# Deformable stage: samples of two 4x4 half blocks side by side on the partitions, and one tile more of lead for the preparation

## The reference, cut to what matters

```python
def deform_conv2d(x, offset, mask, weight):          # K = 3, STRIDE = PAD = 1
    ...
    py = hs + ky + dy                                # row of tap k, plus its offset
    px = ws + kx + dx
    y0 = jnp.floor(py)
    x0 = jnp.floor(px)
    ...
    val = gather(y0i, x0i) * w00 + gather(y0i, x0i + 1) * w01 + gather(y0i + 1, x0i) * w10 + gather(y0i + 1, x0i + 1) * w11
    w_r = weight.reshape(weight.shape[0], weight.shape[1], K2)
    out = jnp.einsum('bkhwc,bkhw,ock->bohw', val, mask, w_r)
    return out
offset = conv2d(x, offset_w, offset_b)
mask = jax.nn.sigmoid(conv2d(x, mask_w, mask_b))
...
x = x + _L1_conv_ref(_gn(x), L1_conv_offset_w, L1_conv_offset_b, L1_conv_mask_w, L1_conv_mask_b, L1_conv_dcn_w)
```

## Time and profile before

| what | us |
|---|---|
| median of 3 runs | 2346.87 |
| the three runs | 2318.73, 2346.87, 2351.54 |
| the profiled execution, its own time | 2314.87 |
| its span | 2313.1 |
| attention, to about | 860 |
| the deformable stage, first spread to last contraction | 911 to 1572 |
| Fourier and FFT convolution | 1583 to 2313 |

### The profile page before, as it was taken

One profiled execution on the slowest core, in us unless ns is written; L12 is line 12 of the kernel. 1 busy time (PEld: TensorE's weight loads), 2 busy tenths in 40 slices (PEclk: granted clock), 3 DMA queues, 4 the chain that ended last, 5 costly groups with the idle time before them and its releaser, 6 DMA issues. The chain is left out here.

```text
span 2313.1 us, 46229 instructions
## 1 busy us (share of the span) xinstructions
PE 2045.3 (88%) x14981; PEld 1256.5 (54%) x14981; DVE 1281.6 (55%) x2688; ACT 1133.4 (49%) x3617; POOL 788.5 (34%) x743
## 2 busy tenths in 40 slices
PE   5699999999999963999999999995694999999999
PEld 3566666666666641232333333324682877777776
DVE  5178888888888871555555555555336222222222
ACT  2378888888888853555555555540121111111111
POOL 0178788787887841222222222210000110110110
PEclk9889999999999985898898998887777999999999
DMA  4300000000000015444444444415002112112110
GB/s 165 110 25 27 26 24 27 26 28 26 26 27 26 24 45 144 123 133 127 121 126 120 123 133 129 108 47 91 10 10 66 34 34 66 33 33 65 34 33 14
DMA packets 169883, 149.70 MB, mean 65 GB/s; under 512 B 60645, under 2 KB 159563, under 8 KB 169694
## 3 DMA queue, kind: packets, MB, share of 16 engines
q1 hardware_dynamic: 169774, 148.38, 24.2%
HBM read 83.68 MB, written 45.89 MB: 56 GB/s over the span
## 5 line engine op out<-in xcount | busy, mean ns | idle before, releaser
L412 ACT ACTIVATE at_probs<-at_sc,at_nmx 128x196 f32<-128x196 f32 x1152 | 473.7, 424 | 116.9 <-DVE at_nmx L358 114.8
L340 POOL TENSOR_TENSOR at_probs<-at_probs,at_rs 128x784 f32<-128x784 f32 x288 | 429.9, 1493 | 156.6 <-DVE at_rs L363 156.6
L447 PE MATMUL at_pt<-at_ident,at_probs 128*98 128x128 f32 x2304 | 312.7, 279 | 40.7 <-DVE at_pts L368 40.1
L358 DVE TENSOR_REDUCE at_nmx<-at_sc 128x4 f32<-128x784 f32 x288 | 277.7, 964 | 124.7 <-PE at_sc L436 124.7
L1237 ACT ACTIVATE dn_mix<-dn_mps 128x432 f32<-128x432 f32 x384 | 182.6, 527 | 297.3 <-PE dn_mps L1139 296.8
L447 PEld LDWEIGHTS at_pt<-at_ident,at_probs 128*98 128x98 f32 x2304 | 242.0, 129 | 142.2 <-POOL at_probs L340 78.6
L436 PE MATMUL at_sc<-at_kw,at_qw 32*128 32x196 f32 x2304 | 273.5, 357 | 12.0 <-POOL at_qw L329 8.0
L1330 DVE COPY dn_sampled<-dn_sps 128x432 f32<-128x432 f32 x192 | 116.7, 608 | 252.3 <-PE dn_sps L1150 251.4
L1139 PE MATMUL dn_mps<-dn_stack,dn_selw 42*128 42x432 f16 x768 | 199.0, 383 | 52.9 <-DMA dn_stack<-near_corners 47.4
L1323 DVE TENSOR_SCALAR dn_mix<-dn_mps 128x432 f32<-128x432 f32 x384 | 213.8, 598 | 44.4 <-PE dn_mps L1139 44.4
L2014 PE MATMUL fc_qps<-fc_wk,fc_xs 99*128 99x128 f32 x1728 | 207.9, 277 | 31.6 <-DMA fc_xs<-in_ones 31.6
(11 more groups left out here) (153 smaller groups left out, 2397.6 us busy)
## 6 DMA issues: line engine op xcount, KB each, us to landing
fc_xs<-fc_xp SPq DMA_DIRECT2D x144, 120.0 KB
dn_slab<-near_image SPq DMA_DIRECT2D x72, 200.0 KB, 3.7
at_vs<-attention_values SPq DMA_DIRECT2D x288, 49.0 KB
near_corners<-dn_split SPq DMA_DIRECT2D x24, 486.0 KB
dn_stack<-near_corners SPq DMA_DIRECT2D x24, 486.0 KB
dn_patch<-near_pixels SPq DMA_DIRECT2D x24, 384.0 KB
attention_values<-ap_vrow SPq DMA_DIRECT2D x21, 256.0 KB, 2.3
near_image<-dn_chunk SPq DMA_DIRECT2D x24, 200.0 KB, 1.9
```

What stands on the lines that cost most here:

```text
L340: nc.gpsimd.tensor_tensor(probs[s][p][:, :, :, :], probs[s][p][:, :, :, :], rs[s][:, 2 * p:2 * p + 2, :].unsqueeze(3).broadcast_to([P, 2, ...
L358: nc.vector.tensor_reduce(nmx[s][:, 2 * p:2 * p + 2, :], sc[p][:, :, 0:2 * NK].rearrange("p b (j k) -> p b j k", j=2), AX.X, ALU.max, nega ...
L412: nc.scalar.activation(probs[s][p][:, b, j, :], sc[p][:, b, NK * j:NK * j + NK], ACT.Exp, bias=nmx[s][:, 2 * p + b, j:j + 1], accum_out=su ...
L447: mm = nc.tensor.transpose(pt[b % 2][0:HK, o:o + P], probs[s][p][:, b % 2, j, HK * c:HK * c + HK], ident[:, :])
```

## The change

The block of 4 x 12 pixels becomes two half blocks of 4 x 4 that share the partitions: partitions 0 to 63 hold the 8 x 8 patch of the left half block, 64 to 127 that of the right one. A tile is then 12 blocks of 8 columns, and a step takes three of them (`PER`), so a tile has 4 steps of 432 columns instead of 8. `stack` has 36 rows of data (18 for each half) over 16 constant rows and is loaded by two DMAs; `spread` still is four matmuls of 432 columns a step. `sample` becomes 3 blocks x 4 images x 2 halves, each a matmul of 64 rows x 32 columns by 144, into two banks `sps0`, `sps1`. `keep` is done for each half. `turn` moves into the bank `cps` of `conv`, with waits between the two. The maps are stored by image and tap, so that one DMA loads all three replicas, and `bias_maps` and `residual` are two instructions each.

The preparation gets one more tile of lead: in tile t, PE convolves tile t+3 in steps 0 and 1 (before: steps 5 to 7), ACT makes the corner weights of t+2 wholly in tile t, `high(t+2)` included (before: `high(t+1)` in step 2), and SP stores the corners of t+1 at the head of its list for tile t (before: at its end).

```diff
-DBW = 12
-DSTEPS = W // DBW
-COLS = TAPS * DR * DBW
-PATCH = (DR + 4) * (DBW + 4)
+HBW = 4
+DBW = 2 * HBW
+NBLK = W // DBW
+PER = 3
+DSTEPS = NBLK // PER
+PX = DR * HBW
+COLS = PER * TAPS * PX
+REACH = HBW + 4
+PATCH = 2 * (DR + 4) * REACH
...
-DATA = 18
-STACK = DATA + DR + 4 + DBW + 4
+DATA = 36
+STACK = DATA + DR + 4 + REACH
...
             def load_patch(j):
...
+                side = (DR + 4) * REACH
+                sp.dma_start(patch[j % 2][0:side, :, :].rearrange("p k n -> p (k n)"),
+                             rows[:, :, 0:NBLK, :].rearrange("r q k n -> (r q) (k n)")).then_inc(patch_in[j % 2], 16)
+                for i in range(2):
+                    sp.dma_start(patch[j % 2][side + i * side // 2:side + (i + 1) * side // 2, :, :].rearrange("p k n -> p (k n)"),
+                                 rows[:, HBW * (1 - i):HBW * (2 - i), i:NBLK + i, :].rearrange("r q k n -> r q (k n)")).then_inc(patch_in[j % 2], 16)
...
             def load_maps(j):
...
-                for a, to in enumerate((hat_y, off_x, mask)):
-                    sp.dma_start(to[:, :], map_d[j % 2, TAPS * a:TAPS * a + TAPS, :, :].rearrange("k b n -> (k b) n").unsqueeze(1).broadcast_to([TAPS * B, 3, DPX])
-                                 ).then_inc(rep_in, 16)
+                sp.dma_start(offs[:, :, :].rearrange("p a n -> p (a n)"),
+                             map_d[j % 2, :, :, :].rearrange("b (k a) n -> (b k) (a n)", a=3).unsqueeze(1).broadcast_to([B * TAPS, 3, 3 * DPX])).then_inc(rep_in, 16)
...
             def load_stack(j):
                 sp.wait_ge(corners_out, 16 * (j + 1))
+                if j >= 1:
+                    sp.wait_ge(stack_in, 32 * j)
...
+                for h in range(2):
+                    sp.dma_start(stack[j % 2][DATA // 2 * h:DATA // 2 * (h + 1), :, :, :, :].rearrange("p b t k n -> p (b t) (k n)"),
+                                 corner_d[j % 2, :, :].rearrange("(g r) (e n) -> (r e) g n", r=3, n=DPX)[:, :, DPX // 2 * h:DPX // 2 * (h + 1)]).then_inc(stack_in, 16)
...
@@ SP, the loop over tiles
             for t in range(DTILES):
                 if t + 1 < DTILES:
+                    store_corners(t + 1)
                     load_patch(t + 1)
+                if t + 1 < DTILES:
+                    load_stack(t + 1)
+                if t + 4 < DTILES:
+                    load_slab(t + 4)
                 save(t)
-                if t + 2 < DTILES:
-                    store_maps(t + 2)
                 if t + 3 < DTILES:
-                    load_slab(t + 3)
+                    store_maps(t + 3)
+                if t + 6 < DTILES:
+                    store_image(t + 6)
+                if t + 3 < DTILES:
+                    load_maps(t + 3)
                 if t + 4 < DTILES:
                     store_pixels(t + 4)
-                if t + 5 < DTILES:
-                    store_image(t + 5)
-                if t + 2 < DTILES:
-                    load_maps(t + 2)
-                if t + 1 < DTILES:
-                    store_corners(t + 1)
-                    load_stack(t + 1)
...
@@ PE
             def turn(g):
...
+                if g >= 2:
+                    pe.wait_ge(maps_ready, 2 * g if g >= 4 else 2 * g - 2)
...
             def sample(s):
...
-                for b in range(B):
-                    mm = nc.tensor.matmul(sps[C * b:C * b + C, 0:COLS], patch[t % 2][:, k, C * b:C * b + C], mix[s % 2][b][:, :], start=True, stop=True)
+                side, n = PATCH // 2, TAPS * PX
+                for i in range(PER):
+                    for b in range(B):
+                        for h in range(2):
+                            mm = nc.tensor.matmul(sps[h][C * b:C * b + C, n * i:n * i + n], patch[t % 2][side * h:side * h + side, PER * k + i, C * b:C * b + C],
+                                                  mix[s % 2][b][side * h:side * h + side, n * i:n * i + n], start=True, stop=True)
...
-                    if k == 0 and t + 4 < DTILES:
+                    if t + 3 < DTILES:
+                        for kx in ((0, 1), (2,), (), ())[k]:
+                            conv(t + 3, kx)
+                    if k == 2 and t + 4 < DTILES:
                         turn(t + 4)
                     if t >= 1:
-                        for tap in range(2 * k - 2, 2 * k):
-                            if 0 <= tap < TAPS:
-                                contract(t - 1, tap)
-                    if t + 3 < DTILES and k >= 5:
-                        conv(t + 3, k - 5)
+                        for tap in ((), (0, 1), (2, 3, 4), (5, 6, 7, 8))[k]:
+                            contract(t - 1, tap)
@@ ACT, in step k of tile t
-                    if t + 2 < DTILES and k == 0:
-                        bias_maps(t + 2)
-                    if t + 1 < DTILES and k == 2:
-                        high(t + 1)
-                    if t + 2 < DTILES and k >= 4:
-                        prepare(t + 2, k - 4)
+                    if k == 1 and t + 3 < DTILES:
+                        bias_maps(t + 3)
+                    if t + 2 < DTILES:
+                        for part in ((0, 1), (2,), (3,), ())[k]:
+                            prepare(t + 2, part)
+                        if k == 3:
+                            high(t + 2)
@@ DVE
-            def keep(s):
+            def keep(s, h):
...
+                nc.vector.tensor_copy(sampled[t % 2][:, :, h, PER * PX * k:PER * PX * (k + 1)].rearrange("p t (k n) -> p t k n", k=PER),
+                                      sps[h][:, 0:COLS].rearrange("p (k t n) -> p t k n", k=PER, t=TAPS)).then_inc(mix_dve, 1)
...
+                    if k == 1 and t + 6 < DTILES:
+                        normalise(t + 6)
+                    if k == 2 and t + 4 < DTILES:
                         keep_rows(t + 4)
-                    if k == 1 and t + 5 < DTILES:
-                        normalise(t + 5)
-                    if k == 2 and t + 2 < DTILES:
-                        largest(t + 2)
-                    keep(s)
-                    if k == 6 and t >= 1:
+                    if k == 3 and t + 3 < DTILES:
+                        largest(t + 3)
+                    for h in range(2):
+                        keep(s, h)
+                    if k == 3 and t >= 1:
                         residual(t - 1)
```

More of the change, by code:

```diff
@@ L949, in stage_deform_near @@
         ident = sb("ident", [P, P])
-        stack = [sb(f"stack{i}", [STACK, TAPS, B, 3 * DR, THIRD], F16) for i in range(2)]
+        stack = [sb(f"stack{i}", [STACK, B, TAPS, NBLK, PX], F16) for i in range(2)]
         stage_stats(nc, "gn1", x_sb, agg,
@@ L1251, in _ @@
             bias_maps(0)
+            prepare(0, 0)
             bias_maps(1)
-            for part in range(4):
+            for part in range(1, 4):
                 prepare(0, part)
             high(0)
+            bias_maps(2)
             for part in range(4):
                 prepare(1, part)
+            high(1)
             for b in (2, 3):
@@ L1347, in _ @@
             largest(1)
+            largest(2)
             for b in range(2):
@@ L1380, in host_l1d @@
     bias = np.zeros((B, C), np.float32)
-    bias[:, 0:27] = np.stack([ob[0::2], ob[1::2], mb]).reshape(27)
+    bias[:, 0:27] = np.stack([ob[0::2], ob[1::2], mb], 1).reshape(27)
     caps = np.zeros((B, C), np.float32)
-    caps[:, 0:18] = 2
+    caps[:, 0:27:3] = 2
+    caps[:, 1:27:3] = 2
     taps = dw.reshape(C, C, TAPS)
@@ L1388, in host_l1d @@
     p = np.arange(PATCH)
-    main = (DR + 4) * DBW
-    r = np.where(p < main, p // DBW, (p - main) // 4)
-    q = np.where(p < main, p % DBW, DBW + (p - main) % 4)
+    side = PATCH // 2
+    u = (p - side) % (side // 2)
+    r = np.where(p < side, p // REACH, u // HBW)
+    q = np.where(p < side, p % REACH, HBW * ((p - side) // (side // 2)) + u % HBW)
     sel = np.zeros((STACK, PATCH), np.float16)
-    for rho in range(3):
-        for half in range(2):
-            for sigma in range(3):
-                sel[6 * rho + 3 * half + sigma, (r % 3 == rho) & (q % 3 == sigma)] = UNIT ** -2
+    for h in range(2):
+        for rho in range(3):
+            for half in range(2):
+                for sigma in range(3):
+                    sel[DATA // 2 * h + 6 * rho + 3 * half + sigma, (p // side == h) & (r % 3 == rho) & (q % 3 == sigma)] = UNIT ** -2
     sel[DATA + r, p] = 1
```

132 lines of the change are left out of this document (65 added, 67 removed).

## The result

The changed kernel takes **2206.95 us** (median of four executions, 2195.37 to 2232.31) against 2336.07 for the kernel before (four executions by then), a ratio of 0.943 with a 95% interval of 0.933 to 0.954. Run again beside the experiments it took 2205.23 (2185.81 to 2224.05), the kernel before 2321.46 in 13 executions there: 0.945 (0.936 to 0.954). Some executions of every kernel are some per cent longer at a lower granted clock; the ratios are taken without them, the medians with them. So it is faster, inside the range, but the forecast was 2130: about three fifths of the expected gain came (129 us between the medians above, 217 forecast).

The account below looks back on a forecast made before the run. PE bounded the old kernel; afterwards the stack chain (17.4 us) plus 0.8 for low clock makes 18.2 us a tile, the stage 437 instead of 644. With 4 for the start, 2112, plus 16 for the median: 2130 us, range 2070 to 2235.

Parts of the forecast that it names:

- TensorE's tile of 15.7 us: PE's work per tile at full clock: spread 3.3, contraction 6.4, convolution 2.0, transposes 0.6, sampling 3.4 us.
- the price by instruction: Rival on sampling: 48 matmuls at 57 ns, 2.7 us a step, PE's tile up to 23.2; chance 0.16 including turn-taking.
- taking turns: Rival on sampling: the two row halves do not overlap, slot 1.6 us, PE's tile 18.7; chance 0.16 including instruction pricing.
- The stack next: With PE's tile shortened, the chain leading to the next stack's load binds; PE waits 1.7 us for each stack.
- 17.4 us: Length of the chain from a tile's first spread through relus, rounding, corner store and stack load to the next tile's.
- SP comes to the store some tenths late: Small addition to the stack chain: the maps load ahead of the corner store waits for corner weights, five pixel stores follow.
- off SP's queue, not off the path: The maps' load as one issue instead of three saves SP 1.6 us, counted as not shortening the stack chain.
- SP's list eats it: No-gain rival: SP's issue list, or a wait between turn and conv, keeps the tile at 26 us, 2317; chance 0.03.
- the packet rival: Stack load priced by packets: 1296 of 384 bytes take 4.5 us longer, chain 21.5, kernel 2209 us; chance 0.12.
- The 16 us for the median: Half of the 32 us between profiled execution and three-run median, added to 2112 to give 2130.
- the rival of a clock that stays at 1.2 GHz: Waits for every stack keep PE's clock low: tile 29.3 us, kernel 2396, 2% over the median; chance 0.04.
- the cheaper case: Rival: the stack chain hides, PE alone sets 15.8 to 16.5 us a tile, about 2080 us; chance 0.10.

Follow-up runs that it names:

- doubled sampling: Against the changed kernel, each sampling matmul is issued twice into the same place; 2205.19 us, ratio 0.952 to the kernel before.
- slab later: Against the changed kernel, SP issues the convolution's slab load just before the maps load, not right behind the stack load; 2161.86 us, ratio 0.931 to the kernel before.
- stack ahead of patch: Against the changed kernel, stack load right behind the corner store, before the patch; rounding before the relus; slab, image and pixel stores moved; 2177.22 us, ratio 0.933.
- all waits covered: Against the changed kernel, rounding before the relus; SP order behind the stack: maps store, image store, slab, save, pixel stores, map load; 2166.89 us, ratio 0.935.

## Why the prediction was right, and where it was short

- **TensorE's tile of 15.7 us**: right. The sampling slot is 0.92 us; the price by instruction (2.7) and taking turns (1.6) are out, and without the stack loads TensorE is busy for 15.7 us a tile at a granted clock of 0.98, in a tile of 16.6. The estimate from the Trainium skill's 60 cycles a matmul ("TensorEngine Tiling (Array Packing)", Performance Considerations), 1.2 us a step, is refuted by the same 0.92.
- **The stack next**: right as to what TensorE waits for, wrong as to why, and mis-sized. The term "17.4 us" took the load at 6.5 us; it is 10.2, and the patch loads, 9 to 12 us behind the stack in the old kernel, now stand right ahead of it; with the stack ahead of them it was 6.8 where TensorE waited. "SP comes to the store some tenths late" is 2.5 us in the tile shown. And the chain is not the bound: cut, it leaves the tile as it was.
- **The failed step** is thus that the sum had no term for SP's queue. I gave its issues away as "off SP's queue, not off the path", though the chain of the earlier trace rows passes through it twice. At 26.8 us a tile it had slack (182.9 us of waiting for TensorE), at 18.2 it had none. The rival "SP's list eats it" named the place, with 26 us too high a price and 0.03 too low a chance.
- **Two terms mis-sized**: the tile of 21.7 us is 17.9 in which TensorE is busy and 3.9 in which it is not. Over the 15.7 at full clock the busy part is 2.2 us, where the forecast had 0.8 for stretches at 1.2 GHz; the rest is the stack, where it had 1.7. But as SP sets the pace, a full clock alone would mostly lengthen the wait: doubled sampling, at a higher clock, left the tile almost as it was.
- **Sum**: 3.4 us a tile too few are 82 us; the first sampling matmul came 9 to 10 us later instead of 4 (3.7 us of that had piled up before the stage, by the end of its statistics). 2112 + 82 + 6 = 2200, and the second profiled execution is 2201.90. The first has the 29 us of the Fourier stretch on top. That 2207 lies in the range is partly luck: the tile of 17 to 19.5 us, which had 0.55, did not come, the upper end of the range was drawn for a dearer sampling, and the packet rival hits the number (2209) by a mechanism that is refuted.
- **The 16 us for the median** were not there: in 13 executions the kernel before has 2321.46, 6.6 above its profiled one, so the three executions lay high.
- **Low clock**: 0.87 granted, against 0.88 before; the rival of a clock that stays at 1.2 GHz is out. So are packets, the cheaper case and no gain. Two readings in these rivals were off, without weight here. "Within some ten us each time" holds in some cases only: in the kernel before TensorE worked at 0.50 from 917 to 943.9 us, busy for 24.9 of the 26.9, and for about 13 us each from 1132 and from 1242. And 17.4 + 4.5 us for packets is 21.9, not 21.5, still without the 0.8 for the clock.

Three variants come out ahead of both kernels, and cannot be told from each other: slab later (0.931), stack ahead of patch (0.933) and all waits covered (0.935). The simplest is one moved call. Their intervals still touch that of the changed kernel (from 0.936), but from first to last sampling matmul they take 457 to 476 us where it takes 519 to 521. Open: whether a second issuing engine for some transfers reaches 16.6 us a tile; that was not run. What share of the 19 to 20 us is the DMA engines' own rate (186 GB/s in the best variant) was not separated from the order either.

## What to carry to other kernels

A queue that issues DMAs in one order and waits for some to land is an engine: sum its issues and waits for a tile before you speed up what it waited for. A landing costs its own bytes and all that was queued ahead, so look at what a reordered list puts right before the transfer that is waited for. When a cut chain changes nothing, look for a second circle of about the same length.

## What the hardware showed that I had not expected

- 48 matmuls with their weight loads, on eight 64x32 tiles of the array, start within 0.71 us, 15 ns apart, and fill a slot of 0.92 us: here the columns set the price, not their number.
- In this load 384-byte packets move in the time of half as many of 768 (6.6 and 6.9 us from issue to use).
- The issue right behind the stack's two DMAs takes longer than elsewhere, whichever it is (medians): slab 3.7 us instead of 1.3, save 2.7 instead of 0.4, maps store 2.3 instead of 1.4. Moving another DMA there moves the cost along.
- The Fourier stretch takes one of two times, 94.7 or about 124 us (once 98.3), at a mean granted clock of 0.73 or 0.53, whatever kernel ran before it. One profile alone would have put 29 us on the change.
- Four times the short matmuls brought stops like the 3.20 us shown inside a run of them, with no semaphore in it.
